# Attention's products with V: split fp32r products step by step, or plain fp32 products in a block per head

## The chip, the cores and the metric

One core of one Trainium2 chip runs the whole program: TensorE (PE) with its weight loads (PEld), VectorE (DVE), ScalarE (ACT), GpSimd (POOL), and SyncE (SP), which issues most DMAs. The metric is the device time of one launch in microseconds (us), as a median of several runs; lower is better.

## The reference

```python
q, k, v = x @ Wq + bq, x @ Wk + bk, x @ Wv + bv          # x: 2048 x 512, 8 heads of 64
scores  = einsum('bdsh,bdth->bdst', q, k) / sqrt(8)
feats   = einsum('bdst,bdth->bdsh', softmax(scores), v)  # the products with V
x1      = layernorm(x + feats @ Wo + bo)
out     = layernorm(x1 + shared_ffn(x1) + routed(x1))    # 64 experts, top 6, capacity 256
```

Everything is fp32.

## The kernel before

The program has four stages: a prologue that makes k, q and v (to about 146 us of the profiled execution), attention (to about 930), the experts, and the sum over each token's six experts with the last layernorm.

Attention runs in chunks of `QC` = 256 queries, 8 chunks of 8 heads. A head (`m`, 64 in all) is four steps (`STEPS`; `u` is the step in the head), and all engines run the same loop over `s`, one iteration a step. The order on each engine is written out by hand. In iteration `s`:

- TensorE turns (transposes, L1696) 4 key tiles x 256 queries of probabilities of the step `r = s - 6` into one of three PSUM slots of 128x1024. It then makes the scores (L1709) of step `s` into the next slot. Turns and scores take the three slots in turn, so scores wait until the slot of the turn before has been read, and a turn waits until the slot of the scores two steps before has been read (`wait_bank`). Behind the scores it makes the products with V (L1736) of the step before the one just turned, into the bank `pv_acc`.
- VectorE reads the turned slot (L1379), then reads the scores' slot into `prob` with a running row minimum (L1398). In `u == 1` it also adds up and inverts the row sums (L1411, L1414).
- ScalarE reads the turned slot (L1027), and applies exp to the scores of three steps ago (L1044).

To keep fp32 precision with fp32r products, v and the turned probabilities are each split in a high part (rounded to fp32r) and a low part (the rest). `v_pair` holds, for each key tile and head, 64 columns of v's high part and 64 of its low part side by side. A key tile takes two products of 256 columns each, with `p_hi` and with `p_lo`. ScalarE makes `p_hi` (two copies of 128x512 a step) and on odd steps one more copy into `prob`. VectorE makes `p_lo` by a subtraction (three in two steps), and GpSimd the fourth (L852) from that copy. The two 64-row halves of `pv_acc` are summed later, after `acc` has been copied (L1018) two steps behind the head's last turn.

Beside this, `chunk_end` of each chunk but the last runs as a job on every engine: `side_step` gives it a turn at two places in each iteration, and `to(n)` says at which turn each piece is done. On VectorE its pieces are the residual, the layernorm (`measure`, L1227 to L1231) and, for each of the chunk's two token tiles, the routing (`mark` L1259, `mark_any` L1268, `find_slots` L1291 to L1297, `sum_top` L1301 and L1303, `keep_weights` L1314, and others).

The experts' down products (L1801) are plain fp32 with 64 weight rows, two experts in the two row halves of the array, four products in a group.

Of the kernel before, what the change touches and what calls it, by code (L numbers as in the profile page):

```python
# [15 lines left out]
P = 128  # L16
# [20 lines left out]
def build(nc, x, x_t, Wq, bq, Wk, bk, Wv, bv, Wo, bo, w_gate, w_sup, w_sdown, w_up, w_down, out):  # L37
# [21 lines left out]
    with ctx:  # L59
# [47 lines left out]
        v_pair = sb("v_pair", [P, NT, H, P], F32R, att)  # L107
# [15 lines left out]
        v_rows = ExitStack()  # L123
        v_gap = sb("v_gap", [P, 2, C], F32, v_rows)
        v_plain = [sb(f"v_plain{i}", [P, 2, C], F32, v_rows) for i in range(2)]
        v_rows.close()
# [6 lines left out]
        p_hi = [sb(f"p_hi{i}", [P, 4, QC], F32R, att) for i in range(2)]  # L133
        p_lo = [sb(f"p_lo{i}", [P, 4, QC], F32R, att) for i in range(2)]
# [10 lines left out]
        class Routing:  # L145
# [72 lines left out]
        g_const, g_lo, g_vlo, g_join, g_bias, g_root, g_count = (sem(f"pool_{n}") for n in (  # L218
            "const", "p_lo", "v_lo", "join", "bias", "root", "count"))
# [5 lines left out]
        a_xhi, a_whi, a_khi, a_qhi, a_vhi = (sem(f"act_{n}") for n in ("x_hi", "w_hi", "k_hi", "q_hi", "v_hi"))  # L225
        a_exp, a_phi, a_copy, a_acc = (sem(f"act_{n}") for n in ("exp", "p_hi", "p_copy", "acc"))
        a_x1t, a_score = sem("act_x1_turned"), sem("act_score")
        a_suphi, a_rhi, a_uphi, a_gate, a_y = (sem(f"act_{n}") for n in ("sup_hi", "rows_hi", "up_hi", "gate", "y"))
        v_xlo, v_wlo, v_klo, v_qlo, v_vadd, v_vlo = (sem(f"dve_{n}") for n in (
            "x_lo", "w_lo", "k_lo", "q_lo", "v_add", "v_lo"))  # L230
        v_min, v_lo, v_sum, v_inv = (sem(f"dve_{n}") for n in ("min", "p_lo", "sum", "inverse"))
# [69 lines left out]
        def wait_bank(e, take, bank):  # L301

            if place_of[take] < 3:
                return
            kind, n = takes[place_of[take] - 3]
            if kind == "k":
                e.wait_ge(v_klo, 2 * n + 2)
            elif kind == "q":
                e.wait_ge(v_qlo, n + 1)
            elif kind == "v":  # L310
                e.wait_ge(v_vadd, n + 1)
            elif kind == "scores":
                e.wait_ge(v_min, n + 1)
            elif kind == "turn" and bank == 0:
                e.wait_ge(v_lo, lo_count(n, 0))
            elif kind == "turn" and n % 2:
                e.wait_ge(a_copy, n // 2 + 1)
            elif kind == "turn":
                e.wait_ge(v_lo, lo_count(n, 1))
# [11 lines left out]
        def lo_count(r, half):  # L331

            return 3 * (r // 2) + (2 if r % 2 else half) + 1
# [58 lines left out]
        def prologue_over(e):  # L392

            e.wait_ge(p_v, NS)
            e.wait_ge(v_vlo, NS)
            e.wait_ge(g_vlo, NS)
            e.wait_ge(a_vhi, 2 * NS)
# [9 lines left out]
        def attention_over(e):  # L407
            e.wait_ge(p_scores, LAST)
            e.wait_ge(p_pv, LAST)
# [347 lines left out]
        def gpsimd(e):  # L757
# [15 lines left out]
            for g in range(NS):  # L773
                e.wait_ge(a_vhi, 2 * g + 2)
                src = v_plain[g % 2][:, 0, :].rearrange("p (h c) -> p h c", h=H)
                e.tensor_tensor(v_pair[:, 2 * g, :, D:P], src, v_pair[:, 2 * g, :, 0:D].bitcast(F32),
                                ALU.subtract).then_inc(g_vlo, 1)
# [69 lines left out]
            for s in range(LAST + LAG + 4):  # L847
                r = s - LAG
                if 0 <= r < LAST and r % 2:
                    m, u = divmod(r, STEPS)  # L850
                    e.wait_ge(a_copy, r // 2 + 1)
                    e.tensor_tensor(p_lo[1][:, 2:4, :], prob[:, m % 2, :, (4 * u + 2) * P:(4 * u + 4) * P],  # L852
                                    p_hi[1][:, 2:4, :].bitcast(F32), ALU.subtract).then_inc(g_lo, 1)
# [67 lines left out]
        def scalar(e):  # L921
# [40 lines left out]
            for g in range(NS):  # L962
                e.wait_ge(v_vadd, g + 1)
                if g == 2:
                    for i in range(2):
                        e.wait_ge(d_qst[i], 32 * (H // 2))
                for t in range(2):
                    e.activation(v_pair[:, 2 * g + t, :, 0:D],
                                 v_plain[g % 2][:, t, :].rearrange("p (h c) -> p h c", h=H),
                                 ACT.Copy).then_inc(a_vhi, 1)  # L970
# [39 lines left out]
            for s in range(LAST + LAG + 4):  # L1010
# [3 lines left out]
                if mj >= 0 and uj == STEPS - 1:  # L1014
                    e.wait_ge(p_pv, STEPS * (mj + 1))
# [124 lines left out]
        def vector(e):  # L1140
# [42 lines left out]
            def add_v(g):  # L1183
                e.wait_ge(p_v, g + 1)
                if g >= 2:
                    e.wait_ge(v_vlo, g - 1)
                    e.wait_ge(g_vlo, g - 1)
                e.tensor_tensor(v_plain[g % 2][:, :, :],
# [3 lines left out]
            def low_v(g):  # L1192
                e.wait_ge(a_vhi, 2 * g + 2)
                e.tensor_tensor(v_pair[:, 2 * g + 1, :, D:P],
                                v_plain[g % 2][:, 1, :].rearrange("p (h c) -> p h c", h=H),
                                v_pair[:, 2 * g + 1, :, 0:D].bitcast(F32), ALU.subtract).then_inc(v_vlo, 1)

            for g in range(NS - V_LATE):
                add_v(g)
                if g < NS - V_LATE - 1:  # L1200
                    low_v(g)
# [167 lines left out]
            for s in range(LAST + LAG + 4):  # L1369
# [3 lines left out]
                if 0 <= r < LAST:  # L1373
                    b = u % 2
# [13 lines left out]
                if s < LAST:  # L1388
# [3 lines left out]
                    if ms >= 2:  # L1392
                        e.wait_ge(p_turned, 2 * ((ms - 2) * 4 + 2 * half + 1) + 2)
                        e.wait_ge(g_lo, ((ms - 2) * 4 + 2 * half + 1) // 2 + 1)
# [7 lines left out]
                if s < V_LATE:  # L1402
                    low_v(NS - V_LATE - 1 + s)
                    add_v(NS - V_LATE + s)
                elif s == V_LATE + 1:
                    low_v(NS - 1)
# [117 lines left out]
        def tensor(e):  # L1524
# [161 lines left out]
            for s in range(LAST + LAG + 4):  # L1686
# [30 lines left out]
                rv = s - LAG - 1  # L1717
                mv, uv = divmod(rv, STEPS)
                if rv >= 0 and rv < LAST:
                    b = uv % 2  # L1720
                    if rv == 0:
                        e.wait_ge(a_vhi, 2 * NS)
                        e.wait_ge(v_vlo, NS)
                        e.wait_ge(g_vlo, NS)
                    if uv == 0 and mv:
                        e.wait_ge(a_acc, mv)
                    for t in range(4):
                        if t % 2 == 0:
                            e.wait_ge(a_phi, 2 * rv + t // 2 + 1)
                            if uv % 2 and t == 2:  # L1730
                                e.wait_ge(g_lo, rv // 2 + 1)
                            else:
                                e.wait_ge(v_lo, lo_count(rv, t // 2))
# [5 lines left out]
                    if uv == STEPS - 1 and mv % H == H - 1 and mv // H < END:  # L1739
                        jobs.append(chunk_end(mv // H))  # L1740
# [155 lines left out]
```

## Time and profile before

| | |
|---|---|
| median of 3 runs | 1277.7 us (1277.64 to 1281.31) |
| profiled execution | 1290.33 us, span 1288.5 us |
| PE busy in the span | 97% |
| DVE, ACT, POOL busy | 77%, 72%, 43% |

The profiled execution is one run, 1% longer than the median. Its page gives each engine's busy time, and the chain of work that ended last, which is followed back from the last instruction to what released each one. A record's duration has the time in it that a matmul takes to drain, so neighbours overlap; the pace of a group is read from the chain, where each piece begins at the end of the last.

### The profile page before, as it was taken

Reading aid. Unit: us, or ns where it says so; the run is one execution under the profiler, and the core shown is the slowest. Engines: PE = TensorE matmul, PEld = TensorE weight load, DVE = VectorE, ACT = ScalarE, POOL = GpSimd, SP = SyncE. Lnnn points to the kernel's source line nnn. Section 1 sums busy time; section 2 is a strip of 40 time slices with the busy share of each in tenths; the row PEclk is TensorE's granted clock in tenths of the full one; section 3 lists DMA queues with packets and bytes.
Section 4 is the critical chain, followed back from the end, with each engine's and each line's share of the span. In section 5 each row is a group of like instructions: output and inputs, shape, how many; then the busy total and the mean of one; then the engine's idle time right before and its main releaser. Section 6 shows DMA issues by size and latency. Waiting matters only on the chain.

```text
span 1288.5 us, 24220 instructions
## 1 busy us (share of the span) xinstructions
PE 1247.3 (97%) x8004; PEld 1049.6 (81%) x8004; DVE 995.9 (77%) x1829; ACT 928.8 (72%) x1643; POOL 560.3 (43%) x570
## 2 busy tenths in 40 slices
PE   7999999999999999999999999999998999999897
PEld 5888799989989889989989989989776777877643
DVE  4723688879979979979979979979876666776378
ACT  5521599969979879978879878979625777877334
POOL 0002233434644643644644553653662656666312
PEclk9999999999999999999999999999999999999899
DMA  8788355434533634444543553573598999897598
GB/s 281 249 294 287 124 137 142 148 110 120 158 93 115 139 111 112 133 127 101 139 130 78 152 134 78 150 208 119 172 353 331 366 363 375 316 311 247 215 427 348
DMA packets 105065, 257.48 MB, mean 200 GB/s; under 512 B 26904, under 2 KB 53464, under 8 KB 101616
## 3 DMA queue, kind: packets, MB, share of 16 engines
q1 hardware_dynamic: 84720, 201.12, 49.8%
q0 software_dynamic: 17920, 50.62, 10.6%
q10 hardware_dynamic: 2304, 4.20, 0.8%
q8 instruction: 68, 1.11, 0.4%
q14 instruction: 53, 0.43, 0.2%
HBM read 182.26 MB, written 134.98 MB: 246 GB/s over the span
## 4 chain that ended last, share of the span: by engine, by line
PE 81%; DVE 9%; issue 6%; DMA 1%; ACT 1%; POOL 1%; another core or an unknown queue 1%; SPq 0%; DVEq 0%; POOLq 0%; ACTq 0%
PE pv_acc L1736 17%; PE slot L1709 17%; PE slot L1696 16%; PE slot L1530 11%; PE misc L1592 4%; PE slot L1801 3%; PE slot L1753 3%; PE slot L1843 3%; PE pv_acc L1530 2%; PE misc L1530 2%; DVE rows_lo L1432 1%; DVE prob L1398 1%; DVE p_lo L1379 1%; DVE up_lo L1467 1%; PE misc L1637 1%
## 5 line engine op out<-in xcount | busy, mean ns | idle before, releaser
L1027 ACT ACTIVATE p_hi<-slot 128x512 fp32r<-128x512 f32 x512 | 279.2, 597 | 107.2 <-PE slot L1696 94.4
L852 POOL TENSOR_TENSOR p_lo<-prob,p_hi 128x512 fp32r<-128x512 f32 x128 | 165.4, 1293 | 364.8 <-ACT prob L1029 364.6
L1379 DVE TENSOR_TENSOR p_lo<-slot,p_hi 128x512 fp32r<-128x512 f32 x384 | 251.6, 683 | 66.3 <-ACT p_hi L1027 64.3
L1709 PE MATMUL slot<-k_stack,q_stack 128*128 128x512 f32 x1024 | 300.3, 415 | 2.2 <-DVE p_lo L1379 2.2
L1044 ACT ACTIVATE prob<-prob,row_min 128x1024 f32<-128x1024 f32 x256 | 297.3, 1161 | 4.0 <-DVE prob L1398 3.8
L1696 PE MATMUL slot<-ident,prob 128*128 128x128 f32 x2048 | 265.9, 273 | 1.3 <-ACT prob L1044 1.3
L1736 PE MATMUL pv_acc<-p_hi,v_pair 128*128 128x256 f32 x1024 | 262.5, 290 | 2.2 <-POOL p_lo L852 2.1
L1736 PE MATMUL pv_acc<-p_lo,v_pair 128*128 128x256 f32 x1024 | 253.9, 281 | 0.0
L1696 PEld LDWEIGHTS slot<-ident,prob 128*128 128x128 f32 x2048 | 228.5, 141 | 1.9 <-issue 1.7
L1736 PEld LDWEIGHTS pv_acc<-p_hi,v_pair 128*128 128x128 f32 x1024 | 192.8, 188 | 15.1 <-issue 3.9
L1736 PEld LDWEIGHTS pv_acc<-p_lo,v_pair 128*128 128x128 f32 x1024 | 192.8, 188 | 13.4 <-issue 3.6
L1709 PEld LDWEIGHTS slot<-k_stack,q_stack 128*128 128x128 f32 x1024 | 173.4, 189 | 27.1 <-issue 3.2
L903 POOL DMA_INDIRECT y_hbm<-y_out,row_at x128 | 141.0, 1102 | 100.6 <-ACT y_out L1080 58.3
L1398 DVE TENSOR_SCALAR_CACHE_REDUCE prob<-slot,row_min 128x1024 f32<-128x1024 f32 x128 | 163.5, 1278 | 0.0
L1398 DVE TENSOR_SCALAR_CACHE_REDUCE prob<-slot 128x1024 f32<-128x1024 f32 x128 | 155.5, 1215 | 0.5 <-PE slot L1709 0.5
L1432 DVE TENSOR_TENSOR rows_lo<-slot,rows_hi 128x1024 fp32r<-128x1024 f32 x69 | 84.4, 1224 | 64.3 <-issue 33.0
L1080 ACT ACTIVATE y_out<-slot 128x1024 f32<-128x1024 f32 x64 | 62.3, 1024 | 45.7 <-PE slot L1801 28.9
L797 POOL DMA_INDIRECT disp_hbm<-resid,scat x84 | 84.0, 1000 | 23.6 <-issue 17.7
L1753 PEld LDWEIGHTS slot<-ident,rows_all 128*128 128x128 f32 x576 | 66.5, 146 | 32.8 <-issue 28.5
L1753 PE MATMUL slot<-ident,rows_all 128*128 128x128 f32 x576 | 79.5, 284 | 5.8 <-DMA rows_all<-disp_hbm 2.8
L1056 ACT ACTIVATE rows_hi<-slot 128x1024 fp32r<-128x1024 f32 x69 | 70.7, 1027 | 16.4 <-PE slot L1753 14.0
L1029 ACT ACTIVATE prob<-slot 128x512 f32<-128x512 f32 x128 | 77.7, 607 | 0.0
(203 smaller groups left out, 1977.1 us busy)
## 6 DMA issues: line engine op xcount, KB each, us to landing
disp_hbm<-zero_hbm SPq DMA_DIRECT2D x64, 518.0 KB, 6.1
rows_all<-disp_hbm SPq DMA_DIRECT2D x64, 518.0 KB
y_hbm<-zero_hbm SPq DMA_DIRECT2D x48, 512.0 KB
got<-y_hbm SPq DMA_DIRECT2D x15, 1536.0 KB, 17.7
q_stack<-q_hbm SPq DMA_DIRECT2D x128, 128.0 KB
up_pair<-in_L_ffn_w_up SPq DMA_DIRECT2D x26, 512.0 KB, 7.1
down_w<-in_L_ffn_w_down SPq DMA_DIRECT2D x32, 256.0 KB
q_hbm<-q_hi SPq DMA_DIRECT2D x8, 512.0 KB, 2.7
```

The lines of the kernel that those rows point to most:

```text
L852: e.tensor_tensor(p_lo[1][:, 2:4, :], prob[:, m % 2, :, (4 * u + 2) * P:(4 * u + 4) * P], p_hi[1][:, 2:4, :].bitcast(F32), ALU.subtract).t ...
L903: e.indirect_dma_start(y_hbm, bass.IndirectOffsetOnAxis(row_at[:, 2 * g + t:2 * g + t + 1], 0), y_out[y][:, t, :], None, bounds_check=T * ...
L1027: e.activation(p_hi[b][:, two, :], view[:, two, :], ACT.Copy).then_inc(a_phi, 1)
L1044: e.activation(keys, keys, ACT.Exp, bias=row_min[:, me % 2, j, 1:2], scale=-1.0, accum_out=row_sum[:, me % 2, j, half:half + 1]).then_inc( ...
L1379: e.tensor_tensor(p_lo[b][:, two, :], view[:, two, :], p_hi[b][:, two, :].bitcast(F32), ALU.subtract).then_inc(v_lo, 1)
L1398: e.tensor_scalar(prob[:, ms % 2, j, half * HALF:(half + 1) * HALF], slot_of_take("scores", s)[:, :], -1.0 / SCALE, first, ALU.mult, ALU.m ...
L1432: e.tensor_tensor(rows_lo[f % LEAD][:, :, :], slot_of_take("flip", f)[:, :].rearrange("p (k q) -> p k q", k=KC), rows_hi[f % LEAD][:, :, : ...
L1530: made = e.matmul(dst, weights[a](k), moving[b](k), start=(k, n) == (0, 0), stop=(k, n) == (KC - 1, 2))
L1696: made = e.transpose(view[:, t, j * P:(j + 1) * P], prob[:, m % 2, j, (4 * u + t) * P:(4 * u + t + 1) * P], ident[:, :])
L1709: made = e.matmul(slot[:, n * BANK:(n + 1) * BANK], qs[:, part, j * P:(j + 1) * P], k_stack[:, ms % H, keys], start=part == 0, stop=part == 1)
L1736: made = e.matmul(pv_acc[:, 0:QC], v_pair[:, kt, mv % H, :], src[:, t, :], start=kt == 0 and part == 0, stop=kt == NT - 1 and part == 1)
L1753: made = e.transpose(view[:, k, t, :], rows[rows_of_item(f)][:, t, k * P:(k + 1) * P], ident[:, :])
```

## The change

The change drops the high and low parts. v is kept once as fp32 in `v_all` (2 KB a key tile and partition where `v_pair` has 4). The turned probabilities are copied as they are into `p_t`, of which there are two sets of four (one for each step of a head): ScalarE copies the first two key tiles of a step, VectorE the last two. The four sorts of instruction that made low parts, the extra copy, and the splitting of v in the prologue go. The products with V are plain fp32: 64 weight columns, 256 moving columns. Even key tiles go to PSUM rows 0 to 63, odd ones to rows 64 to 127, which are the two column halves of the array. All 16 of a head stand in one block, in the same iteration as the head's last turn, behind its scores. A product of fp32 is two records in the trace (a pass each), one of fp32r is one.

```diff
@@ scalar: a turned step
-                    b = u % 2
-                    if r >= 2:
-                        e.wait_ge(p_pv, r - 1)
-                    for half in range(2):
-                        two = slice(2 * half, 2 * half + 2)
-                        e.wait_ge(p_turned, 2 * r + half + 1)
-                        e.activation(p_hi[b][:, two, :], view[:, two, :], ACT.Copy).then_inc(a_phi, 1)
-                    if u % 2:
-                        e.activation(prob[:, m % 2, :, (4 * u + 2) * P:(4 * u + 4) * P], view[:, 2:4, :],
-                                     ACT.Copy).then_inc(a_copy, 1)
+                    if m >= 2:
+                        e.wait_ge(p_pv, m - 1)
+                    e.wait_ge(p_turned, 2 * r + 1)
+                    e.activation(p_t[m % 2][u][:, 0:2, :], view[:, 0:2, :], ACT.Copy).then_inc(a_pt, 1)
@@ vector: a turned step
-                    for half in range(2 - u % 2):
-                        two = slice(2 * half, 2 * half + 2)
-                        e.wait_ge(a_phi, 2 * r + half + 1)
-                        e.tensor_tensor(p_lo[b][:, two, :], view[:, two, :], p_hi[b][:, two, :].bitcast(F32),
-                                        ALU.subtract).then_inc(v_lo, 1)
+                    if m >= 2:
+                        e.wait_ge(p_pv, m - 1)
+                    e.wait_ge(p_turned, 2 * r + 2)
+                    e.tensor_copy(p_t[m % 2][u][:, 2:4, :], view[:, 2:4, :]).then_inc(v_pt, 1)
@@ tensor: the products with V
-                if rv >= 0 and rv < LAST:
-                    b = uv % 2
-                    if uv == 0 and mv:
-                        e.wait_ge(a_acc, mv)
-                    for t in range(4):
-                        ...
-                        kt = 4 * uv + t
-                        for part, src in enumerate((p_hi[b], p_lo[b])):
-                            made = e.matmul(pv_acc[:, 0:QC], v_pair[:, kt, mv % H, :], src[:, t, :],
-                                            start=kt == 0 and part == 0, stop=kt == NT - 1 and part == 1)
-                    made.then_inc(p_pv, 1)
+                if 0 <= r < LAST and u == STEPS - 1:
+                    if m == 0:
+                        e.wait_ge(v_vadd, NS)
+                    else:
+                        e.wait_ge(a_acc, m)
+                    for kt in range(NT):
+                        if kt % 4 == 0:
+                            e.wait_ge(a_pt, STEPS * m + kt // 4 + 1)
+                        elif kt % 4 == 2:
+                            e.wait_ge(v_pt, STEPS * m + kt // 4 + 1)
+                        half = slice(kt % 2 * D, (kt % 2 + 1) * D)
+                        made = e.matmul(pv_acc[half, 0:QC], v_all[:, kt, m % H * D:(m % H + 1) * D],
+                                        p_t[m % 2][kt // 4][:, kt % 4, :], start=kt < 2, stop=kt >= NT - 2)
+                    made.then_inc(p_pv, 1)
```

On TensorE, in the middle of attention, one step of the program before reads as follows; each step has its turn (`slot<-ident,prob`), its scores, and eight products with V, and every other step is the same.

```order
L1696 MATMUL slot<-ident,prob 128x128 x8
L1709 MATMUL slot<-k_stack,q_stack 128x512 x4
L1736 MATMUL pv_acc<-p_hi,v_pair 128x256
L1736 MATMUL pv_acc<-p_lo,v_pair 128x256
L1736 MATMUL pv_acc<-p_hi,v_pair 128x256
L1736 MATMUL pv_acc<-p_lo,v_pair 128x256
L1736 MATMUL pv_acc<-p_hi,v_pair 128x256
L1736 MATMUL pv_acc<-p_lo,v_pair 128x256
L1736 MATMUL pv_acc<-p_hi,v_pair 128x256
L1736 MATMUL pv_acc<-p_lo,v_pair 128x256
```

At the same place of the changed program a whole head stands between two blocks of products with V.

```order
L1674 MATMUL pv_acc<-p_t,v_all 64x256 x16
L1642 MATMUL slot<-ident,prob 128x128 x8
L1655 MATMUL slot<-k_stack,q_stack 128x512 x4
L1642 MATMUL slot<-ident,prob 128x128 x8
L1655 MATMUL slot<-k_stack,q_stack 128x512 x4
L1642 MATMUL slot<-ident,prob 128x128 x8
L1655 MATMUL slot<-k_stack,q_stack 128x512 x4
L1642 MATMUL slot<-ident,prob 128x128 x8
L1655 MATMUL slot<-k_stack,q_stack 128x512 x4
L1674 MATMUL pv_acc<-p_t,v_all 64x256 x16
```

The turns and scores of four steps now follow one another with nothing between, and the products of the four steps stand together behind the last.

On VectorE, during a chunk's routing, the program before has these rows; they are the steps `u` = 3, 0 and 1 of a head (`x_t` and `small` are the routing's tiles).

```order
L1398 TENSOR_SCALAR prob,row_min<-slot 128x1024
L1249 MAX top<-score 128x8
L1251 MAX_INDEX top_i<-top,score 128x8
L1253 CAST small<-top_i 128x6
L1379 TENSOR_TENSOR p_lo<-slot,p_hi 128x512 x2
L1398 TENSOR_SCALAR prob,row_min<-slot,row_min 128x1024
L1259 TENSOR_TENSOR x_t<-iota_e,small 128x384
```

In the changed program the same steps, and the two after them, read so.

```order
L1201 MAX top<-score 128x8
L1203 MAX_INDEX top_i<-top,score 128x8
L1205 CAST small<-top_i 128x6
L1330 COPY p_t<-slot 128x512
L1347 TENSOR_SCALAR prob,row_min<-slot,row_min 128x1024
L1211 TENSOR_TENSOR x_t<-iota_e,small 128x384
L1330 COPY p_t<-slot 128x512
L1347 TENSOR_SCALAR prob,row_min<-slot,row_min 128x1024
L1357 TENSOR_TENSOR row_inv<-row_sum 128x2
L1360 RECIPROCAL row_inv<-row_inv 128x2
L1220 TENSOR_REDUCE picked<-x_t 128x64
L1330 COPY p_t<-slot 128x512
```

Each step has one copy where it had one or two subtractions. The row sums and the routing's pieces stay in the steps in which they were, between the reads of the slots.

## Rows read from the trace of the kernel before

**Rows 1.** The page: span, and the engines' busy times.

```profile
span 1288.5 us, 24220 instructions
PE 1247.3 (97%) x8004; PEld 1049.6 (81%) x8004; DVE 995.9 (77%) x1829; ACT 928.8 (72%) x1643; POOL 560.3 (43%) x570
```

**Rows 2.** Chain of work that ended last, 400 to 412 us: start, duration, what.

```profile
402.82 0.87 PE slot L1696 x8
403.70 0.93 PE slot L1709 x4
404.63 0.95 PE pv_acc L1736 x8
```

**Rows 3.** Waits of PE, 200 to 800 us: total, times, longest.

```profile
PE slot L1709 <- DVE p_lo L1379: 2.2, 3, 0.7
```

**Rows 4.** Chain of work, whole span: plain fp32 in the experts and at attention's end.

```profile
456.91 3.43 PE misc L1592 x8
...
929.32 1.05 PE misc L1614 x2
...
1087.35 1.92 PE slot L1801 x8
1089.26 1.03 PE slot L1753 x8
```

**Rows 5.** Chain of work, 1085 to 1100 us: eight transposes away from such a group.

```profile
1085.05 0.87 PE slot L1753 x8
```

**Rows 6.** Timeline of DVE, 402.5 to 408.3 us: start, duration, line, operation.

```profile
402.08 0.67 DVE L1379 TENSOR_TENSOR p_lo<-slot,p_hi 128x512 fp32r<-128x512 f32 x1
402.67 1.27 DVE L1398 TENSOR_SCALAR_CACHE_REDUCE prob<-slot,row_min 128x1024 f32<-128x1024 f32 x1
...
403.87 0.16 DVE L1291 TENSOR_SCALAR small<-small 128x6 f32<-128x6 f32 x1
...
404.22 0.68 DVE L1379 TENSOR_TENSOR p_lo<-slot,p_hi 128x512 fp32r<-128x512 f32 x1
...
406.02 0.29 DVE L1411 TENSOR_TENSOR row_inv<-row_sum 128x2 f32<-128x2 f32 x1
...
406.43 0.14 DVE L1301 TENSOR_REDUCE small<-top 128x1 f32<-128x6 f32 x1
...
406.74 1.29 DVE L1379 TENSOR_TENSOR p_lo<-slot,p_hi 128x512 fp32r<-128x512 f32 x2
```

**Rows 7.** Timeline of all engines, 400 to 406 us: a turn, scores, ScalarE's copies and exp.

```profile
402.66 1.03 PE L1696 MATMUL slot<-ident,prob 128*128 128x128 f32 x8
...
403.36 1.09 ACT L1027 ACTIVATE p_hi<-slot 128x512 fp32r<-128x512 f32 x2
...
403.45 1.18 PE L1709 MATMUL slot<-k_stack,q_stack 128*128 128x512 f32 x4
...
404.81 1.16 ACT L1044 ACTIVATE prob<-prob,row_min 128x1024 f32<-128x1024 f32 x1
...
405.85 0.21 ACT L1044 ACTIVATION_READ_ACCUMULATOR prob<-prob,row_min 128x1 f32 x1
```

**Rows 8.** Groups of DVE by line: busy us, mean ns, idle before.

```profile
L1268 DVE TENSOR_REDUCE picked<-x_t 128x64 bf16<-128x384 f32 x15 | 12.8, 850 | 0.0
...
L1227 DVE BATCH_NORM_STATS2 moments<-resid 128x6 f32<-128x512 f32 x14 | 9.7, 691 | 0.0
...
L1314 DVE SCALAR_TENSOR_TENSOR weight_of<-small,top 128x6 f32<-128x6 f32 x15 | 9.2, 616 | 0.1
...
L1259 DVE TENSOR_TENSOR x_t<-iota_e,small 128x384 f32<-128x384 f32 x15 | 8.3, 554 | 0.0
...
L1229 DVE BATCH_NORM_AGGREGATE moments<-moments 128x2 f32<-128x6 f32 x16 | 2.9, 182 | 0.5
```

**Rows 9.** Chain of work, 90 to 170 us: the prologue's end.

```profile
89.95 43.52 PE slot L1530 x187
```

**Rows 10.** Chain of work, 924 to 938 us: attention's end.

```profile
927.43 1.89 PE pv_acc L1736 x16
```

More of the change, by code:

```diff
@@ L106, in build @@
         early.close()
-        v_pair = sb("v_pair", [P, NT, H, P], F32R, att)
+        v_all = sb("v_all", [P, NT, C], F32, att)
+        p_over_x = [sb(f"p_t1{u}", [P, 4, QC], F32, att) for u in range(4)]
+        sb("unused", [P, 4 * BANK * 2], F32, att)
         wo_sb = sb("wo_sb", [P, KC, C], F32, att)
@@ L122, in build @@
         w_hi[0], w_lo[0] = (sb(name, [P, KC, C], F32R, pro) for name in ("w_hi0", "w_lo0"))
[L123 to L126, printed above, removed]
         w_hi[1], w_lo[1] = (sb(name, [P, KC, C], F32R, pro) for name in ("w_hi1", "w_lo1"))
@@ L132, in build @@
         prob = sb("prob", [P, 2, QT, T], F32, att)
-        p_hi = [sb(f"p_hi{i}", [P, 4, QC], F32R, att) for i in range(2)]
-        p_lo = [sb(f"p_lo{i}", [P, 4, QC], F32R, att) for i in range(2)]
+        p_t = [[sb(f"p_t0{u}", [P, 4, QC], F32, att) for u in range(4)], p_over_x]
         q_stack = [sb(f"q_stack{i}", [P, 2, QC], F32R, att) for i in range(2)]
@@ L215, in build @@
         f_rstd, f_shift = (hid[0][:, 44 + i * NT:44 + (i + 1) * NT] for i in range(2))
-        g_const, g_lo, g_vlo, g_join, g_bias, g_root, g_count = (sem(f"pool_{n}") for n in (
-            "const", "p_lo", "v_lo", "join", "bias", "root", "count"))
+        g_const, g_join, g_bias, g_root, g_count = (sem(f"pool_{n}") for n in (
+            "const", "join", "bias", "root", "count"))
         g_wlo, g_froot, v_uplo = sem("pool_up_lo"), sem("pool_final_root"), sem("dve_up_lo")
@@ L224, in build @@
         p_flip, p_up, p_down = (sem(f"pe_{n}") for n in ("rows_turned", "up", "down"))
-        a_xhi, a_whi, a_khi, a_qhi, a_vhi = (sem(f"act_{n}") for n in ("x_hi", "w_hi", "k_hi", "q_hi", "v_hi"))
-        a_exp, a_phi, a_copy, a_acc = (sem(f"act_{n}") for n in ("exp", "p_hi", "p_copy", "acc"))
+        a_xhi, a_whi, a_khi, a_qhi = (sem(f"act_{n}") for n in ("x_hi", "w_hi", "k_hi", "q_hi"))
+        a_exp, a_pt, a_acc = (sem(f"act_{n}") for n in ("exp", "p_turned", "acc"))
         a_x1t, a_score = sem("act_x1_turned"), sem("act_score")
         a_suphi, a_rhi, a_uphi, a_gate, a_y = (sem(f"act_{n}") for n in ("sup_hi", "rows_hi", "up_hi", "gate", "y"))
-        v_xlo, v_wlo, v_klo, v_qlo, v_vadd, v_vlo = (sem(f"dve_{n}") for n in (
-            "x_lo", "w_lo", "k_lo", "q_lo", "v_add", "v_lo"))
-        v_min, v_lo, v_sum, v_inv = (sem(f"dve_{n}") for n in ("min", "p_lo", "sum", "inverse"))
+        v_xlo, v_wlo, v_klo, v_qlo, v_vadd = (sem(f"dve_{n}") for n in ("x_lo", "w_lo", "k_lo", "q_lo", "v_add"))
+        v_min, v_pt, v_sum, v_inv = (sem(f"dve_{n}") for n in ("min", "p_turned", "sum", "inverse"))
         v_resid, v_norm = sem("dve_resid"), sem("dve_norm")
@@ L313, in wait_bank @@
                 e.wait_ge(v_min, n + 1)
[L314 to L317, printed above, removed]
             elif kind == "turn":
-                e.wait_ge(v_lo, lo_count(n, 1))
+                e.wait_ge((a_pt, v_pt)[bank], n + 1)
             elif kind == "flip":
@@ L329, in wait_bank @@
                 y_made(e, n - SH)
-        def lo_count(r, half):
-            return 3 * (r // 2) + (2 if r % 2 else half) + 1
         def low_by_dve(g):
@@ L394, in prologue_over @@
             e.wait_ge(p_v, NS)
-            e.wait_ge(v_vlo, NS)
-            e.wait_ge(g_vlo, NS)
-            e.wait_ge(a_vhi, 2 * NS)
+            e.wait_ge(v_vadd, NS)
             e.wait_ge(g_const, 5)
@@ L408, in attention_over @@
             e.wait_ge(p_scores, LAST)
-            e.wait_ge(p_pv, LAST)
+            e.wait_ge(p_pv, NCH * H)
         def head_out(e, m):
@@ L772, in gpsimd @@
                             pattern=[[1, P]], channel_multiplier=-1).then_inc(g_const, 1)
[L773 to L777, printed above, removed]
             prologue_over(e)
@@ L847, in gpsimd @@
             for s in range(LAST + LAG + 4):
[L848 to L853, printed above, removed]
                 side_step(jobs)
@@ L961, in scalar @@
                              bias=bias_q[:, pair:pair + 1]).then_inc(a_qhi, 1)
[L962 to L970, printed above, removed]
             constants_in(e)
@@ L1014, in scalar @@
                 if mj >= 0 and uj == STEPS - 1:
-                    e.wait_ge(p_pv, STEPS * (mj + 1))
+                    e.wait_ge(p_pv, mj + 1)
                     if mj:
@@ L1184, in add_v @@
                 e.wait_ge(p_v, g + 1)
[L1185 to L1188, printed above, removed]
+                if g == NS // 2:
+                    for i in range(2):
+                        e.wait_ge(d_qst[i], 32 * (H // 2))
+                e.tensor_tensor(v_all[:, 2 * g:2 * g + 2, :],
                                 slot_of_take("v", g)[:, :].rearrange("p (t n) -> p t n", t=2),
                                 bv_all.unsqueeze(1).to_broadcast([P, 2, C]), ALU.add).then_inc(v_vadd, 1)
[L1192 to L1196, printed above, removed]
             for g in range(NS - V_LATE):
                 add_v(g)
-                if g < NS - V_LATE - 1:
-                    low_v(g)
             constants_in(e)
@@ L1373, in vector @@
                 if 0 <= r < LAST:
-                    b = u % 2
                     view = slot_of_take("turn", r)[:, :].rearrange("p (t q) -> p t q", t=4)
-                    for half in range(2 - u % 2):
-                        two = slice(2 * half, 2 * half + 2)
-                        e.wait_ge(a_phi, 2 * r + half + 1)
-                        e.tensor_tensor(p_lo[b][:, two, :], view[:, two, :], p_hi[b][:, two, :].bitcast(F32),
-                                        ALU.subtract).then_inc(v_lo, 1)
+                    if m >= 2:
+                        e.wait_ge(p_pv, m - 1)
+                    e.wait_ge(p_turned, 2 * r + 2)
+                    e.tensor_copy(p_t[m % 2][u][:, 2:4, :], view[:, 2:4, :]).then_inc(v_pt, 1)
                 mv, uv = divmod(s - LAG - 1, STEPS)
@@ L1393, in vector @@
                         e.wait_ge(p_turned, 2 * ((ms - 2) * 4 + 2 * half + 1) + 2)
-                        e.wait_ge(g_lo, ((ms - 2) * 4 + 2 * half + 1) // 2 + 1)
                     if half:
@@ L1402, in vector @@
                 if s < V_LATE:
-                    low_v(NS - V_LATE - 1 + s)
                     add_v(NS - V_LATE + s)
-                elif s == V_LATE + 1:
-                    low_v(NS - 1)
                 if 0 <= r < LAST and u == 1:
@@ L1716, in tensor @@
                     project_pairs(0)
-                rv = s - LAG - 1
-                mv, uv = divmod(rv, STEPS)
-                if rv >= 0 and rv < LAST:
-                    b = uv % 2
[L1721 to L1724, printed above, removed]
-                    if uv == 0 and mv:
-                        e.wait_ge(a_acc, mv)
-                    for t in range(4):
[L1728 to L1733, printed above, removed]
-                        kt = 4 * uv + t
-                        for part, src in enumerate((p_hi[b], p_lo[b])):
-                            made = e.matmul(pv_acc[:, 0:QC], v_pair[:, kt, mv % H, :], src[:, t, :],
-                                            start=kt == 0 and part == 0, stop=kt == NT - 1 and part == 1)
+                if 0 <= r < LAST and u == STEPS - 1:
+                    if m == 0:
+                        e.wait_ge(v_vadd, NS)
+                    else:
[8 more added lines that the diff above has]
+                                        p_t[m % 2][kt // 4][:, kt % 4, :], start=kt < 2, stop=kt >= NT - 2)
                     made.then_inc(p_pv, 1)
-                    if uv == STEPS - 1 and mv % H == H - 1 and mv // H < END:
-                        jobs.append(chunk_end(mv // H))
+                mv, uv = divmod(s - LAG - 1, STEPS)
+                if mv >= 0 and uv == STEPS - 1 and mv % H == H - 1 and mv // H < END:
+                    jobs.append(chunk_end(mv // H))
                 side_step(jobs)
```

## The prediction

> **What bounds the kernel now.** I read the page first: TensorE is busy 97% of the span, VectorE 77%, ScalarE 72% [rows 1]. A busy share doesn't prove a bound, so next the chain of work that ended last, in the middle of attention. There the reader is to see three pieces that follow each other with no gap, all TensorE's: eight transposes 0.87 us, four scores 0.93, eight products with V 0.95 [rows 2]. A step is 2.75 us, a head of four steps 11.0, and products with V are 4 x 0.95 = 3.80 of it. The waits agree: in 600 us TensorE waited 2.2 us in all [rows 3]. So attention is worth what TensorE's work costs, and the other engines' work costs nothing while it fits under 2.75 us a step.
>
> **The products themselves.** Before, a head has 32 fp32r records at 0.95 / 8 = 0.119 us. After, it has 16 fp32 products of two records each, again 32. What a plain fp32 record costs stands in the output projection: 8 records of 512 columns in 3.43 us, 0.429 each, so 0.2145 for 256 columns [rows 4]. One after the other, 32 of them would be 6.86 us. What matters is whether the two column halves run side by side. No row shows column halves. The nearest are the experts' down products, 64-row weights in the two row halves: 8 records of 512 columns in 1.92 us, where the same number over the whole array took 3.43. A lone 64-row product (2 records) took 1.05, no less than the 0.86 of a whole one, so the gain comes from the pair and not from the half array [rows 4]. Four pairs at 0.429 are 1.72; the other 0.20 is paid on entering the half-array form. The eight transposes behind the group take 1.03 where they take 0.87 elsewhere, 0.16 on leaving [rows 4, 5]. I take the column halves to do as the row halves do: 16 x 0.2145 + 0.20 + 0.16 = 3.79 us a head, against 3.80. That is a gain of 0.01 x 64 = 1 us: nothing. The new form trades a faster stream (0.107 a record against 0.119) for a switch that costs the same. The bounds are 3.43 with no cost of switching (-23 us over 64 heads) and 6.86 + 0.36 with no pairing (+219). Between them lies a smaller doubt: two fp32 streams read as many bytes per unit of time as one fp32r stream, and the fp32r one runs at 0.119 and not 0.107. If that is the price of reading, the block is 11% longer, +0.37 us a head, +23.
>
> **What the block does to the order.** Here is where I expect the loss. Before, each step gave TensorE 2.75 us of work while VectorE did its part. After, turns and scores of four steps come back to back at 0.87 + 0.93 = 1.80 us a step, and 3.79 us of products stand behind them. TensorE works in program order, so when a turn or scores have to wait for a slot, the block behind them can't fill the gap. VectorE's part of a step: the read of the scores starts 1.20 us before what follows it, a 128x512 subtraction from PSUM 0.59 [rows 6]. The copy that replaces the subtraction is not in the trace. It reads the same 512 elements from PSUM, and the read of the scores, which like it has one source, needs 1.20 for 1024, so I take 0.60. Below, it could be half, if a plain copy ran at twice the pace; above, nothing suggests more. A step is then 1.80 us on VectorE too: exactly TensorE's pace, with no room. Now the chain through a head, from the first turn at 0. The scores of `u` = 0 begin at 0.87 and are in PSUM 1.18 later [rows 7], 2.05; VectorE reads them until 3.25, copies turn 1 until 3.85, reads scores 1 until 5.05, adds and inverts the row sums (0.41, from 406.02 to 406.43 in [rows 6]) until 5.46, copies turn 2 until 6.1. The scores of `u` = 3 need that copy, and TensorE wants to begin them at 3 x 1.80 + 0.87 = 6.27. So in a head without side work there is 0.1 to 0.2 us to spare (I take 0.12), and no stall. All that VectorE does between those reads in addition comes straight out of TensorE's time.
>
> The Trainium skill (VectorE: DVE Perf Modes, Mode 2x_2P) lets a one-source fp32 operation run at twice the pace only where source and destination are both in SBUF. By that rule the copy from PSUM stays at 0.60 and the stalls below at 31 us; at half the time they would be 11. The 1.20 us for 1024 elements from PSUM agrees; no row shows a plain copy.
>
> The chunk's jobs do just that. By their `to(n)` (two turns an iteration, counted from the first iteration behind the head) these pieces fall behind the read of `u` = 0, or in `u` = 1, or ahead of `u` = 2's copy: `measure` of the first tile 0.87 us (0.69 + 0.18), `mark` 0.55 and `mark_any` 0.85 in one head for each tile, `keep_weights` of the second tile 0.62 [rows 8], and in one head for each tile `find_slots` 0.35 (403.87 to 404.22) with `sum_top` 0.31 (406.43 to 406.74) [rows 6]. The other pieces fall in `u` = 3 or behind `u` = 2's copy, with the block as cover, or wait for a product of TensorE's own. Less 0.12 in each head: 0.75 + 2 x 1.28 + 2 x 0.54 + 0.50 = 4.9 us a chunk, 34 for the seven chunks. The groups' means hold about 0.07 us that overlaps the next instruction (1.27 against 1.20 in [rows 6]), some 3 us in all: 31 us. Before the change these same pieces cost nothing, since a step left VectorE about 0.9 us.
>
> **What costs nothing.** ScalarE's second copy and its copy for GpSimd, GpSimd's subtraction and a third of VectorE's go, but TensorE was not waiting for them [rows 3]. ScalarE's new step is one copy, about 0.5 (two take 1.09), and 1.25 of exp (404.81 to 406.06) [rows 7]: 1.75 against 1.80. It also starts on the first half of a turn, so it stays ahead; without that lead its 0.05 a step to spare would be gone. Splitting v in the prologue goes too, under TensorE's unbroken 43.5 us of products [rows 9]. The last head's products were partly spread over its steps; 16 records (1.89 us) stood alone at the end [rows 10], and now all 32 do: +2 us. The block doesn't wait for `u` = 3's copies, which it needs only for its last quarter, nor does the copy of `pv_acc`, still two steps later.
>
> **The sum.** -1 + 31 + 2 = +32 us. The profiled execution is 1290.3 and would be 1322; the median of the runs is 1277.7, which gives 1310. Its own range: half of the side work passing through (+16), up to all of it with the slower stream (+32 + 23, and a few for the row sums being late): 1293 to 1338.
>
> **The rivals.** *Switching is free.* If column halves are entered and left with nothing paid, the block is 3.43 and gives back 23 us: 1287. It ends on the other side only if VectorE's stalls are under 21 us. With a copy at half time the chain above has 0.12 + 0.6 to spare, which leaves 0.15 + 2 x 0.68 = 1.5 us a chunk, 11 in all: -24 + 11 + 2, 1267. Against it speak the 0.20 and 0.16 at the row halves; for it, that only 64 columns have to be loaded before the first product. If only the stalls are absent and the switch is paid, 1279, no change. Together 0.2.
>
> *The weights of one half are not loaded under the other half's stream.* Both halves share all rows, which the row halves of the trace don't. Of the 1.05 us of the lone product, 0.19 is more than its two passes need [rows 4]; if about 0.1 of that were a weight load that is exposed at each of the 16 passes, the block would be 1.6 us longer: +102, 1412, and half of it 1361. Against it speaks that products over the whole array, which share all rows too, follow each other at 1.89 / 16 = 0.118 us with no such 0.1 added [rows 10].
>
> The Trainium skill (TensorE: Matmul & The Clock Gate, What overlaps and what doesn't) says that a weight load overlaps a running matmul only when its row group differs; by that the block would be about 5.4 us and the kernel near 1412. Its section on LDWEIGHTS also names a background buffer, which would spare it. No row of this trace decides for column halves. Chance 0.1.
>
> *No pairing at all.* 7.22 us a head, +219, 1529. Nothing in the trace excludes it, but the row halves did pair. Chance 0.09.
>
> **How the numbers follow.** The forecast 1310 has 0.61. The range is to reach from the faster rival to the middle of the exposed loads: 1267 to 1375 leaves out no pairing (0.09), the upper part of exposed loads (0.06) and a little at the lower end. About 0.3% is what a measurement of this kernel can tell from no change. Faster by more: 0.13, the free switch with short stalls. Within: 0.08, the absent stalls. Slower: 0.79.
>
> **What would show it.** In the chain of the changed kernel, eight transposes and four scores at 1.80 us a step; the 32 records of products with V in 3.6 to 3.9 us, in pairs that start together, the transposes behind them at about 1.03 us. The waits of TensorE should have new rows, scores waiting for the copy into `p_t` and turns for the read of the scores, 30 us in all and nearly all inside chunks' routing. Wrong would be: records that follow one another at 0.21, a block over 4.5 us, steady heads of more than 11.1 us without side work, or no waits of TensorE for VectorE.

## The result, and the profile after

The changed kernel takes 1288.7 us (median of 4 runs), the kernel before 1277.7. The ratio is 1.0079, 95% interval 1.0061 to 1.0098: slower by 11 us where 32 were forecast.

The page of the changed kernel first: the span, the busy times, and the two groups that are new, with busy us, mean ns, and idle time before.

```profile
span 1286.7 us, 23210 instructions
PE 1243.3 (97%) x8004; PEld 927.9 (72%) x8004; DVE 889.9 (69%) x1693; ACT 721.3 (56%) x1243; POOL 381.4 (30%) x434
...
L1330 DVE COPY p_t<-slot 128x512 f32<-128x512 f32 x256 | 175.1, 684 | 165.7 <-PE slot L1642 164.5
...
L1674 PE MATMUL pv_acc<-p_t,v_all 128*64 128x256 f32 x2048 | 235.2, 382 | 0.0
```

VectorE, ScalarE and GpSimd lost 8 to 16 points of busy share against [rows 1], and TensorE has as many records as before, 8004. The profiled execution of the changed kernel is 1288.5 us, like its median. That of the kernel before was 1% above its median, so the two spans can't be compared as wholes. Attention can, since most of its heads of one sort repeat to 0.03 us.

The chain of work over one head with little side work, to hold against [rows 2]: start, duration, what.

```profile
404.41 1.02 PE slot L1642 x8
405.43 0.92 PE slot L1655 x4
406.36 0.87 PE slot L1642 x8
407.23 0.92 PE slot L1655 x4
408.15 0.87 PE slot L1642 x8
409.02 0.92 PE slot L1655 x4
409.94 0.00 issue
409.94 1.06 PE slot L1642 x8
411.00 0.93 PE slot L1655 x4
411.93 3.60 PE pv_acc L1674 x32
```

Turns and scores follow at 1.79 us, the block of 32 records takes 3.60, and the transposes behind it 1.02 where others take 0.87. The turn of `u` = 3 takes 1.06 here: it waits a little, because this head has `find_slots` in it. The waits of TensorE over attention (total, times, longest) show where it stands still:

```profile
PE misc L1593 <- DVE picked L1220: 13.7, 13, 1.1
PE slot L1642 <- ACT prob L1004: 2.0, 2, 1.3
```

L1593 is the first product of `rank`, and `picked` is what `mark_any` writes. This wait is not in [rows 3], and the prediction did not name it. The chain around one of the 13, where VectorE's pieces take over from TensorE's:

```profile
429.74 0.89 PE slot L1642 x8
...
430.99 0.08 DVE prob L1347
431.07 0.47 DVE x_t L1211
431.54 0.08 DVE p_t L1330
...
432.06 1.28 DVE prob L1347 x2
433.34 0.09 DVE row_inv L1357
...
433.53 0.83 DVE picked L1220
434.36 0.05 issue
434.40 0.20 PE misc L1593
434.61 0.03 PE misc L1594
434.64 0.94 PE slot L1642 x8
```

To be seen is the forecast's chain through VectorE: scores read, `mark` (L1211), a copy, scores read, row sums, `mark_any` (L1220). What it ends at is `rank`, which stands on TensorE behind the scores of `u` = 2, ahead of the turn of `u` = 3.

The length of each head, from its first transpose to the next head's, gives the account. Heads are named by what TensorE or VectorE does beside them in a chunk (those beside the first chunk's end stand here); us.

| head | before | after | rank later (e1) | pieces moved (e5) |
|---|---|---|---|---|
| no side work | 11.01 | 10.95 | 10.95 | 10.95 |
| output projection, first tile; `measure` follows | 14.45 | 14.41 | 14.38 | 14.38 |
| output projection, second tile | 14.47 | 14.40 | 14.40 | 14.40 |
| x1 turned, gate, first tile | 12.31 | 12.26 | 12.26 | 12.26 |
| `mark`, `mark_any`, rank, first tile | 11.12 | 12.36 | 11.65 | 11.09 |
| `find_slots`, `sum_top`, first tile | 11.01 | 11.13 | 11.13 | 10.97 |
| x1 turned, gate, second tile | 12.32 | 12.25 | 12.25 | 12.31 |
| `mark`, `mark_any`, rank, second tile | 11.12 | 12.32 | 11.84 | 11.04 |
| `find_slots`, `sum_top`, second tile | 11.01 | 11.13 | 11.15 | 10.95 |
| all heads but the last | 762.4 | 775.1 | 766.7 | 756.5 |

### The profile page after: what moved, and what is told of

Read it like the earlier page. It is cut to its first block, busy times and chain, and to the rows that moved or that the text cites. A ratio compares the mean times of both kernels' runs of the same rounds, so it can differ in the third digit from the quotient of the medians.

```text
span 1286.7 us, 23210 instructions
## 1 busy us (share of the span) xinstructions
PE 1243.3 (97%) x8004; PEld 927.9 (72%) x8004; DVE 889.9 (69%) x1693; ACT 721.3 (56%) x1243; POOL 381.4 (30%) x434
## 4 chain that ended last, share of the span: by engine, by line
PE 88%; DVE 5%; DMA 3%; issue 2%; POOL 1%; ACT 0%; SPq 0%; DVEq 0%; POOLq 0%; ACTq 0%
PE pv_acc L1674 18%; PE slot L1642 17%; PE slot L1655 16%; PE slot L1476 11%; PE slot L1740 5%; PE slot L1692 5%; PE misc L1538 4%; PE pv_acc L1476 3%; PE misc L1476 3%; PE slot L1782 2%; DMA got<-y_hbm 2%; DVE prob L1347 1%; DVE picked L1220 1%; PE misc L1583 1%; DVE base L1437 1%
## 5 line engine op out<-in xcount | busy, mean ns | idle before, releaser
L1004 ACT ACTIVATE prob<-prob,row_min 128x1024 f32<-128x1024 f32 x256 | 293.3, 1146 | 69.1 <-DVE prob L1347 62.5
L990 ACT ACTIVATE p_t<-slot 128x512 f32<-128x512 f32 x256 | 151.7, 592 | 293.1 <-PE slot L1642 291.4
L1330 DVE COPY p_t<-slot 128x512 f32<-128x512 f32 x256 | 175.1, 684 | 165.7 <-PE slot L1642 164.5
L1642 PE MATMUL slot<-ident,prob 128*128 128x128 f32 x2048 | 269.3, 275 | 2.0 <-ACT prob L1004 2.0
L1674 PE MATMUL pv_acc<-p_t,v_all 128*64 128x256 f32 x2048 | 235.2, 382 | 0.0
L1674 PEld LDWEIGHTS pv_acc<-p_t,v_all 128*64 128x64 f32 x2048 | 141.5, 137 | 90.8 <-issue 26.3
L844 POOL TENSOR_TENSOR moved<-acc,moved 64x256 f32<-64x256 f32 x63 | 46.0, 730 | 530.5 <-DMA moved<-acc 530.4
L1740 PE MATMUL slot<-down_w,hid 64*128 64x512 f32 x256 | 64.9, 615 | 1.2 <-DVE hid L1405 1.2
L1476 PE MATMUL slot<-x_hi,w_hi 128*128 128x512 f32 x128 | 52.2, 408 | 7.3 <-DVE x_lo L1111 7.3
L1476 PE MATMUL slot<-x_lo,w_hi 128*128 128x512 f32 x128 | 52.3, 408 | 0.0
```

What stands on the lines that cost most here:

```text
L990: e.activation(p_t[m % 2][u][:, 0:2, :], view[:, 0:2, :], ACT.Copy).then_inc(a_pt, 1)
L1004: e.activation(keys, keys, ACT.Exp, bias=row_min[:, me % 2, j, 1:2], scale=-1.0, accum_out=row_sum[:, me % 2, j, half:half + 1]).then_inc( ...
L1330: e.tensor_copy(p_t[m % 2][u][:, 2:4, :], view[:, 2:4, :]).then_inc(v_pt, 1)
L1476: made = e.matmul(dst, weights[a](k), moving[b](k), start=(k, n) == (0, 0), stop=(k, n) == (KC - 1, 2))
L1642: made = e.transpose(view[:, t, j * P:(j + 1) * P], prob[:, m % 2, j, (4 * u + t) * P:(4 * u + t + 1) * P], ident[:, :])
L1674: made = e.matmul(pv_acc[half, 0:QC], v_all[:, kt, m % H * D:(m % H + 1) * D], p_t[m % 2][kt // 4][:, kt % 4, :], start=kt < 2, stop=kt >= ...
```

## The experiments

The kernel before was timed beside each. It took 1292.3 us on the chip of e1 to e4 and 1281.0 on that of e5 to e7, so ratios to it are compared, and times in attention from the traces.

**e1: rank half an iteration later on TensorE.**

```diff
                 for j, start in ((0, P0), (1, P1)):
                     ...
-                    yield from to(start + 14)
+                    yield from to(start + 15)
                     rank(c, j)
```

> The changed kernel with the two products of rank half an iteration later on TensorE (behind the scores of u = 3, not behind those of u = 2). Theory: most of the loss is TensorE waiting for mark_any (13.7 us at the rank products in the changed kernel's trace). The same lateness of VectorE then shows in part at the slots of u = 3, about 0.6 us in each of 14 heads instead of 1.2: 1280 us, 1277 to 1283. If nothing takes its place: 1275. Rival, the forecast's own chain (the slots are late by all of VectorE's pieces, the wait at rank only stands in for them): 1286 or more.

Ratio 1.0011 (0.9990 to 1.0033). The heads but the last are 8.5 us shorter than after, 766.7 against 775.1. About 9 us had been expected of this theory, 13.7 if nothing took the wait's place, at most 3 by the rival. The two heads with `mark_any` are 0.5 to 0.7 us shorter and still 0.5 to 0.7 us longer than before the change (in the other chunks both take about 11.65, but for one of 12.20). The chain shows the rest of the wait, now at the second half of the scores of `u` = 3, which needs VectorE's copy:

```profile
431.50 0.68 DVE p_t L1330
432.19 0.04 issue
432.23 0.73 PE slot L1655 x2
```

**e2: e1, and scores wait for both copies of the turned slot at once.**

```diff
             elif kind == "turn":
-                e.wait_ge((a_pt, v_pt)[bank], n + 1)
+                e.wait_ge(a_pt, n + 1)
+                e.wait_ge(v_pt, n + 1)
```

> The kernel of e1_rank_late, but scores wait for both copies of the turned slot before their first half, which is how the forecast read the code; in the changed kernel the first half waits for ScalarE's copy alone. Theory: the forecast overcounted since VectorE's copy is needed 0.46 us later than it reckoned: 5 to 12 us above e1_rank_late. Rival, VectorE's copy is early enough either way: within 2 us of it.

Ratio 1.0118 (1.0083 to 1.0152), and 779.9 us in attention: 13.2 above e1 (the medians differ by 14.7), a little over what was expected. Heads with `mark_any` rose from 11.65 to 12.19, those with `find_slots` from 11.13 to 11.5, and heads without side work stayed at 10.95, but for two at 11.3. Against the 10.95 to 10.97 that e5 below has, the heads with `find_slots` lose 0.5, which is the 0.54 of the forecast. So the forecast had its chain right for a code that waits like this one. The real one gives VectorE's copy two scores' time, 0.46 us, more. The list of waits puts 8.6 us of e2 down to ScalarE, but that is its copy of the next turn: in the first head with `mark_any` it ends at 300.10, when TensorE's weight load has begun (300.09), and VectorE's copy had ended at 299.97.

**e3: the products step by step, in column halves.**

```diff
-                if 0 <= r < LAST and u == STEPS - 1:
-                    ...
-                    for kt in range(NT):
+                rv = r - 1
+                if 0 <= rv < LAST:
+                    mp, up = divmod(rv, STEPS)
+                    ...
+                    for kt in range(4 * up, 4 * up + 4):
```

> The changed kernel with its products with V step by step, four in each step and one step behind the turn, as before the change, and not 16 in a block. Theory: a switch into column halves and back costs 0.30 us, paid four times a head and not once: +58 us, less some 17 us of waits for VectorE that go: 1320 to 1335. Rival, switching costs nothing and only the block makes TensorE wait: 1268 to 1275.

Ratio 1.0365 (1.0329 to 1.0401), 46 us above the kernel before. The expectation of 1320 to 1335 was 42 to 57 above the 1277.7 of the first chip, so this lies in it, though the 1338.1 itself doesn't. The chain has every step alike:

```profile
400.64 1.02 PE slot L1642 x8
401.67 0.94 PE slot L1655 x4
402.60 1.01 PE pv_acc L1677 x8
403.62 1.02 PE slot L1642 x8
```

Eight records at the block's pace (3.60 less the entry, over 16 pairs: 0.216 a pair) are 0.86; they take 1.01, and the transposes behind them 1.02 instead of 0.87. A switch costs 0.15 going in and 0.15 coming out. A head is 11.89 us, 0.94 more than with one block, which is three more switches. TensorE's waits for VectorE are gone here too: the heads with `mark_any` are 11.94.

**e4: even key tiles first, then odd ones.**

```diff
-                    for kt in range(NT):
+                    for kt in [*range(0, NT, 2), *range(1, NT, 2)]:
```

> The changed kernel with the same 16 products of a head, but the eight even key tiles first and then the eight odd ones, so that neighbours share a column half. Theory: halves run side by side only when neighbours in program order lie in different halves; the block is 32 records at 0.216 us, 6.9 us, and the kernel 1495 to 1515 us. Rival, each half has a queue of its own deep enough to pair the eight with the eight: the block stays at 3.6 us and the kernel near 1289. Between: a queue of some records pairs those around the middle and the kernel is 20 to 60 us under 1505.

1468.7 us, one run, where the kernel before took 1292.3 on that chip. The block in the chain:

```profile
405.88 6.24 PE pv_acc L1674 x32
```

It is 2.64 us longer than 3.60, and that in each head: 13.58 against 10.95. This is the middle case. Without any pairing 32 records at 0.216 and the entry of 0.15 would be 7.06, so 0.82 us is saved, the time of nearly four records. The starts of the records in the trace say which: twelve of the even half follow one another at 0.216, then the first of the odd half starts 0.006 us behind the thirteenth, and the next three start 0.056 us behind the last three of the even half. The other twelve of the odd half follow alone. So a record started beside another half's only when three records or fewer of that half still stood ahead of it, and the kernel's alternating order is what makes the block short.

**e5: VectorE's side pieces moved.**

```diff
-                for tick, part in ((6, score_experts), (8, choose), (10, mark), (12, mark_any), (15, pick_rank),
-                                   (16, write_codes), (17, find_place), (19, find_slots), (21, sum_top), (23, share)):
+                for tick, part in ((6, score_experts), (8, choose), (9, mark), (9, mark_any), (15, pick_rank),
+                                   (16, write_codes), (17, find_place), (17, find_slots), (22, sum_top), (23, share)):
                 ...
-                yield from to(P1 + 4)
+                yield from to(P1 + 6)
                 keep_weights(c, 0)
```

> The changed kernel with VectorE's side pieces moved to where the block of products with V covers them: mark and mark_any at the start of u = 0, find_slots beside find_place there, sum_top and the first tile's keep_weights behind the copy of u = 2. TensorE's order is untouched. Theory: TensorE's waits for VectorE in attention (1.2 us in two heads of a chunk, 0.18 in two more) go, 2.8 us a chunk, 19 us in all; heads without side work stay at 10.95 us: ratio to the changed kernel 0.985, about 8 us under the kernel before (0.993). Rival, the loss is in the block form itself (switches, shorter steps) and not in where VectorE's pieces stand: no more than 5 us under the changed kernel.

Ratio 0.9940 (0.9917 to 0.9962): 7.5 us faster than the kernel before, 17 faster than the changed one on the same chip (1273.5 against 1290.9). The waits of TensorE in attention:

```profile
PE slot L1642 <- ACT prob L1004: 2.0, 2, 1.3
PE misc L1555 <- DVE x_t L1231: 0.4, 1, 0.4
```

The wait at rank is gone, and so are those at the slots (the table's last column). Attention's heads take 18.7 us less than in the changed kernel, 16.2 of it in the heads with `mark_any`, 2.1 in those with `find_slots` and 0.6 in those with the second tile's `keep_weights`. TensorE's work and its order are the same in both, so what the block form loses on the way is the standing of these pieces.

**e6: the same moves in the kernel before.** The diff is that of e5.

> The kernel before with the same pieces moved on VectorE. Theory: there TensorE's steps of 2.75 us cover the pieces wherever they stand, so nothing changes: 0.998 to 1.002 of the kernel before. Rival, the pieces cost something there too and moving them is a gain of its own: 0.995 or less.

Ratio 1.0017 (0.9998 to 1.0036), no gain and by the trace a small loss: the head with `mark` and `mark_any` of the second tile is 11.48 us or more where it was 11.12, since the two pieces together are now more than a step of 2.75 us covers. The moves pay only with the block.

**e7: the changed kernel again.**

> The changed kernel once more, unaltered, on the same chip as the two above, so that their distance to it is measured on one chip: 1.006 to 1.010 of the kernel before, by the first comparison.

Ratio 1.0079 (1.0054 to 1.0104), the same as at first; 775.5 us in attention's heads (775.1).

## Why the prediction was wrong

The direction and the mechanism held: slower, because turns and scores of four steps come with nothing between them and VectorE's side pieces reach TensorE. The size did not: +11 us measured, +32 forecast. The step that failed is the term of 31 us for those pieces, and after it the tail.

**The side pieces: 31 forecast, 18.7 measured** (changed kernel against e5, the same products and the same order on TensorE; e5 leaves `measure` and the second tile's `keep_weights` where they were). By piece:

- `measure`, 0.75 us a chunk forecast: nothing. Its head is 14.40 us long, and 10.95 with 3.43 would be 14.38. In `u` = 1 of this head TensorE has the second tile's output projection, 3.43 us, by the same kind of tick. The prediction saw this cover for the addition behind `measure` and not for `measure` itself.
- `mark` with `mark_any`, 1.28 in each of two heads: 1.27 and 1.28. That the size agrees is luck, since it arises at another place. TensorE waits 1.1 us at rank, which needs `mark_any`'s result and stands before the turn of `u` = 3. The prediction listed which slots VectorE would release late and did not ask who takes the pieces' own results. With rank later (e1) the wait at the slots is 0.56 and 0.80 (11.65 and 11.84 against e5), and not 1.28, for the reason of the next point.
- `find_slots` with `sum_top`, 0.54 in each of two heads: 0.16 and 0.18. VectorE's copy of `u` = 2 is needed by the second half of the scores of `u` = 3 and not by the first, 0.46 us later than reckoned. This is in `wait_bank`, where the scores' first bank waits for `a_pt` and the second for `v_pt`. e2 takes that room away and the head loses 0.37 more. What is left is the wait of the turn of `u` = 3 for the read of the scores of `u` = 1, seen in the chain of the result.
- `keep_weights` of the second tile, 0.50 in each of seven chunks: 0.27, 0.21 and 0.10 in three of the six heads that have it, nothing in the others (14.65, 14.62 and 14.48 against 14.38 to 14.41). The piece itself takes 0.14 to 0.17 us. Its mean of 0.62 in [rows 8] was a mixture: in the kernel before it took either 0.15 or 1.12 to 1.22. In the three slow heads it was the addition of the row sums just ahead of it that was long, 0.79 to 0.97 us for 0.16.

Over the seven chunks the four terms were forecast at 5, 18, 8 and 3.5 us, 34 in all, less 3 for overlap. They measured 0, 16.2, 2.1 and 0.6. The forecast's cost of `mark` was about right, and the others were read as waits of TensorE where it had cover, room or nothing to wait for.

The long records in the last point share a cause that the prediction left out. Each ends when an elementwise instruction of GpSimd ends, as here in the kernel before, where the two ends are 355.25 and 355.26:

```profile
353.95 1.30 POOL L783 TENSOR_TENSOR resid<-resid,bo_all 128x512 f32<-128x512 f32 x1
...
354.13 1.13 DVE L1314 SCALAR_TENSOR_TENSOR weight_of<-small,top 128x6 f32<-128x6 f32 x1
```

In attention the kernel before has 78 such long records of the routing and the row sums. All end within 0.06 us of GpSimd's, 58 of them with its subtraction L852, which the change removes; the changed kernel has 25. A group's mean hides such a pair of durations; the timeline shows it.

**The last head: +2 forecast, -3.8 measured.** From its first transpose to its last product it takes 11.2 us where it took 15.0. The chain of the changed kernel's end, against [rows 10]:

```profile
931.33 0.93 PE slot L1642 x8
932.26 2.79 PE misc L1555 x6
935.06 3.60 PE pv_acc L1674 x32
```

The block stands alone as predicted, 3.60 against 1.89. But the row of before was read without what precedes it: there the chain ran through VectorE, while TensorE waited, for GpSimd's part of `p_lo` (L852) among others. From the chain, and from the waits of TensorE over 146 to 930 us:

```profile
914.99 1.92 DVE small L1253
916.90 1.03 issue
917.93 1.06 DVE p_lo L1379 x2
...
920.28 1.59 DVE row_inv L1411
```

```profile
PE pv_acc L1736 <- POOL p_lo L852: 2.1, 2, 1.6
```

The subtractions that the change removes did have a price in this one head, where nothing covered them, GpSimd's above all. TensorE waited 2.1 us for its results, and GpSimd held up two short instructions of VectorE: the row sums at L1411 took 1.66 us for 0.16, under L852, and the cast at L1253 3.03 for 0.17, under L852 and the instructions before and behind it. Which share of the 3.8 us is whose, no run separates. "Cost nothing" had been read off the middle of attention.

**The products: -1 forecast, about -6 measured.** A head without side work went from 11.01 to 10.95 us, 4 us over the kernel, mostly since entering the column halves costs 0.15 and not the row halves' 0.20 (e3). The rest lies in single heads, e5 against before: three of the kernel before took 12.14 us, which are the waits of [rows 3], with VectorE's L1291 held up by GpSimd's subtraction (1.19 to 1.21 us for 0.16) in each of them. That is 3.4 us, and the first head gives back 0.9, since before the change it had three steps' products with V and not four. Pairing in the column halves, taken over from the row halves, was right: 16 x 0.216 + 0.15 + 0.15 = 3.75 against 3.79.

The sum in attention: -6 + 18.7 - 3.8, and 0.3 by which it starts later, are +9.2 us. The forecast had +32 from the same three terms. The traces have the last product with V at 929.04 before and at 938.28 after. The medians differ by 11.0. The rest, 1.8 us, lies outside attention or in the spread of the runs; the runs don't settle which.

**The rivals.** *Switching is free* fell with e3. The stalls were under the 21 us that it named, but the switch is paid. *Weights not loaded under the stream* and *no pairing* fell with the block of 3.60 us. The Trainium skill (TensorE: Matmul & The Clock Gate, What overlaps and what doesn't) lets a weight load overlap a running matmul only when its row group differs. The column halves share all rows, and 16 pairs with their loads took 3.60 us: by the prediction's estimate that rule would have given 5.4. The Trainium skill (TensorE: Matmul & The Clock Gate, Step-by-step: what each phase is for) also allows the overlap where the load goes to the background weight buffer, and with that the block agrees.

That the copy from PSUM takes as long as the subtraction was right: 684 ns a record against 683 for the subtraction, 0.60 from one start to the next (443.65 to 444.25).

```profile
443.57 0.17 DVE L1249 TENSOR_TENSOR scat<-small 128x6 uint32<-128x6 f32 x1
443.65 0.69 DVE L1330 COPY p_t<-slot 128x512 f32<-128x512 f32 x1
444.25 1.27 DVE L1347 TENSOR_SCALAR_CACHE_REDUCE prob<-slot,row_min 128x1024 f32<-128x1024 f32 x1
445.45 0.08 DVE L1347 DVE_READ_ACCUMULATOR prob<-slot,row_min 128x1 f32 x1
445.45 0.15 DVE L1357 TENSOR_TENSOR row_inv<-row_sum 128x2 f32<-128x2 f32 x1
```

## What to carry to other kernels

When work that was spread evenly over an in-order engine is gathered in a block, its total may stay the same, but the stretch between blocks becomes shorter than the other engines' part. List what they do in that stretch, with two questions for each piece: which buffer it releases late, and who waits for its result. Then move these pieces under the block, before judging the block: here that turned 11 us lost into 7.5 us gained, and the same moves without the block gained nothing. Read each wait at the bank or half that it guards, and take "costs nothing" from the stretch in question, the last one too.

## What the runs showed of the hardware

Plain fp32 products in the two column halves of TensorE run in pairs, 0.216 us for two records of 256 columns, if neighbours in program order lie in different halves. With eight products and eight, the time of nearly four records of 32 was saved: 6.24 us against 7.06. So TensorE does start a record of the other half ahead of its turn, but here no more than three records ahead. Going into column halves costs 0.15 us and coming back to the whole array 0.15, each time (e3).

Some of VectorE's short instructions depend on what GpSimd does. The addition of the row sums (2 columns), `keep_weights`, the cast and the scalings of the routing (6 columns) take 0.15 to 0.23 us alone. Where they start under an addition, subtraction or product of GpSimd over 256 or 512 columns, they end with it, after 0.28 to 1.7 us and once after 3.03. The reciprocals don't: in the kernel before 31 of those of the row sums start under an instruction of GpSimd, and none is longer. Nor does GpSimd's power of a single column (0.57 us) hold anything up, in seven cases.
